# A pre-norm transformer block on one core: the softmax shift is added by two bf16 matmuls instead of four fp32r ones

## The chip, the cores and the metric

The kernel runs on one core of a Trainium2 chip. The metric is the device time of one execution in microseconds (us); lower is better. The engines are named as in the profile: PE (TensorE, matmuls), PEld (its weight loads), DVE (VectorE), ACT (ScalarE), POOL (GpSimd), SP (SyncE, which issues DMAs). Each engine runs its own instructions in program order and waits on semaphores for the others.

## What is computed

Input x is 8 sequences of 1024 positions with 128 features. Two sublayers follow each other, each on a layer norm of x and added to it.

```python
def _L0_attn_ref(x, Wq, Wk, Wv, Wo):        # 16 heads of 8, window of 64
    q = split_heads(x @ Wq); k = split_heads(x @ Wk); v = split_heads(x @ Wv)
    ...                                      # each query sees itself and the 63 keys before it
    scores = jnp.einsum('bhld,bhlwd->bhlw', q, k_win) * scale
    scores = jnp.where(invalid[None, None, :, :], -jnp.inf, scores)
    attn = jax.nn.softmax(scores, axis=-1)
    ctx = jnp.einsum('bhlw,bhlwd->bhld', attn, v_win)
    ...
    return ctx @ Wo

def _L0_ffn_ref(x, w_router, w1, w2, bias):  # 8 experts, top 2, capacity 2048 per expert
    scores = jax.nn.softmax(xf @ w_router, axis=-1)
    expert_weights, top_experts = jax.lax.top_k(scores, TOP_K)
    ...                                      # rows are gathered by expert, in order, up to the capacity
    h = jax.nn.gelu(jnp.einsum('ech,ehf->ecf', xb, w1))
    y = jnp.einsum('ecf,efh->ech', h, w2).reshape(E * capacity, hs)
    ...
    return out.reshape(sl, bs, hs) + bias

x = x + _L0_attn_ref(_layernorm(x), Wq, Wk, Wv, Wo)
x = x + _L0_ffn_ref(_layernorm(x), w_router, w1, w2, bias)
```

What matters here is the softmax. It is computed as exp(score - maximum), and the maximum has to be known before the exp.

## The kernel before

**Stages.** The eight sequences go through attention one after the other; each is eight tiles of 128 positions, and one tile is one *slot* (`slot(b, t)` on PE, DVE, ACT and POOL alike; `g` is 8b + t). Beside the slots of sequence b run the second layer norm, the routing and the scatter of sequences b-1 to b-3, cut in small steps (`small` on DVE, `sends` on POOL). After the last slot come the routing of the last sequences and then the experts, in a loop of their own.

**Units.** A slot has two *units* u = 2g and 2g+1, one for each group of 8 heads. The scores of a unit are in two PSUM banks, `sT_ps[:, u % 2, 0:2, :]`, transposed: keys in the partitions, and 1024 columns, one for each pair of query and head (128 queries, 8 heads). A unit goes through these steps:

1. `fill` (PE, L1089 and L1095; L1085 for the first tile of a sequence): a bf16 mask matmul pair writes 0 or a large negative number for the window, and four fp32 matmuls add the scores. `sT_ps` stays open for accumulation.
2. `part_max` (DVE, L675): a transposing reduce takes the maxima over blocks of 32 keys, into `kmax`, 128x32.
3. `maxima_T` (PE, L1104): two matmuls against the identity transpose `kmax` twice, to PSUM partitions 0 to 31 and 32 to 63 of `maxima_ps`.
4. `shifts` (DVE): a reduce over the key blocks with its sign turned gives `negmax` (L681), 64x32: the negative maximum of each query column, in the row of its block of queries and heads. Then `moving` (L684) is `negmax` times the 0/1 mask `blocks`, so that row c holds only the 32 columns of its own block c.
5. `shifted` (PE, L1114): four fp32r matmuls, each with 32 rows, add `moving` to the open scores. The weights `chosen` are 0/1 and pick which 8 of a bank's 16 rows go to which half of the bank, so each of them covers 256 columns.
6. `exps` (ACT, L508): exp of the two banks into `probsT`.
7. `weighted` (PE, L1124): eight matmuls with four column groups give the weighted sums and the denominators; then ACT copies them, PE transposes them (`weighted_T`, L1133), DVE divides (`normalise`, L692, L697), and PE transposes and projects (`context_T` L1138, `project` L1142). DVE adds the residual (L703).

**Order.** All orders are written out by hand. PE in a slot: `shifted(2g)`, `weighted` of the previous slot, `project`, the projections or norm transposes of a later pair, `maxima_T(2g+1)`, `fill` of unit 2g+2, `shifted(2g+1)`, `weighted`, `weighted_T`, `maxima_T(2g+2)`, in odd slots `values` (L1075), `fill` of unit 2g+3, `context_T`. DVE: `part_max(2g+1)`, side steps, residual, `shifts(2g+1)`, `part_max(2g+2)`, side steps, `normalise`, `shifts(2g+2)`. Buffers `moving`, `kmax`, `maxima_ps` and `sT_ps` are double, by u % 2.

The shift in code:

```python
for j in range(2):
    for b in range(2):
        rows = slice(b * STRIP, (b + 1) * STRIP)        # STRIP = 32
        last = mm(sT_ps[:, u % 2, b, j * 2 * P:(j + 1) * 2 * P], chosen[rows, j, :],
                  moving[rows, u % 2, :, :].rearrange("p c q -> p (c q)"),
                  start=False, stop=True, skip_group_check=True)
```

Of the kernel before, what the change touches and what calls it, by code (L numbers as in the profile page):

```python
# [5 lines left out]
F32R = mybir.dt.float32r  # L6
BF16 = mybir.dt.bfloat16
I32 = mybir.dt.int32
U32 = mybir.dt.uint32
ALU = mybir.AluOpType  # L10
ACT = mybir.ActivationFunctionType
AX = mybir.AxisListType
# [7 lines left out]
P = 128  # L20
# [8 lines left out]
HALF = P // 2  # L29
UNIT = 2 * 512  # L30
STRIP = 32
# [17 lines left out]
def moe_block_kernel(nc, x, wq, wk, wv, wo, w_router, w1, w2, bias, out):  # L49
    ctx = ExitStack()  # L50
    with ctx:
        def sb(name, shape, dt=F32):
            return ctx.enter_context(nc.sbuf_tensor(name, shape, dt))
# [4 lines left out]
        def sem(name):  # L58
            return ctx.enter_context(nc.semaphore(name))
# [17 lines left out]

        eighth = sb("eighth", [HALF, 8])
        blocks = sb("blocks", [HALF, 8, 32])
        eights = sb("eights", [HALF, 2])  # L80
        chosen = sb("chosen", [HALF, 2, P], F32R)
# [27 lines left out]
        negmax = sb("negmax", [HALF, 32])  # L109

        moving = sb("moving", [HALF, 2, 8, 32], F32R)
# [54 lines left out]
        d_rden = sem("d_rden")  # L166
        d_groups = sem("d_groups")
# [449 lines left out]
        def _(dve):  # L617
# [60 lines left out]
            def shifts(u):  # L678

                dve.wait_ge(s_maxT, u + 1)  # L680
                nc.vector.tensor_reduce(negmax[:, :], maxima_ps[u % 2][0:HALF, MAXIMA:MAXIMA + P].rearrange("p (k q) -> p q k", q=32),  # L681
                                        AX.X, ALU.max, negate=True).then_inc(s_negmax, 1)
                dve.wait_ge(s_negmax, u + 1)
                nc.vector.tensor_tensor(out=moving[:, u % 2, :, :],  # L684
                                        in0=negmax[:, :].unsqueeze(1).to_broadcast([HALF, 8, 32]),
                                        in1=blocks[:, :, :],
                                        op=ALU.mult).then_inc(s_moving, 1)
# [123 lines left out]
            for t in range(2):  # L811
# [14 lines left out]


            nc.vector.tensor_reduce(eighth[:, :], ident[0:HALF, 0:HALF].rearrange("p (x c) -> p c x", c=8),
                                    AX.X, ALU.max).then_inc(d_groups, 1)
            nc.vector.tensor_reduce(eights[:, :], ident[0:HALF, 0:96].rearrange("p (x r) -> p x r", x=2)[:, :, 0:16]  # L830
                                    .rearrange("p x (j c) -> p j x c", j=2), AX.XY, ALU.max).then_inc(d_groups, 1)
            dve.wait_ge(d_groups, 2)
            nc.vector.tensor_copy(blocks[:, :, :], eighth[:, :].unsqueeze(2).to_broadcast([HALF, 8, 32]))
            nc.vector.tensor_copy(chosen[:, :, :], eights[:, :].unsqueeze(2).to_broadcast([HALF, 2, P]))
# [222 lines left out]
        def _(pe):  # L1057
# [42 lines left out]
            def maxima_T(u):  # L1100

                pe.wait_ge(s_kmax, u + 1)
                for b in range(2):
                    last = mm(maxima_ps[u % 2][STRIP * b:STRIP * (b + 1), MAXIMA:MAXIMA + P], kmax[:, u % 2, :], ident[:, :],  # L1104
                              start=True, stop=True)
                last.then_inc(s_maxT, 1)

            def shifted(u):

                pe.wait_ge(s_moving, u + 1)  # L1110
                for j in range(2):
                    for b in range(2):
                        rows = slice(b * STRIP, (b + 1) * STRIP)
                        last = mm(sT_ps[:, u % 2, b, j * 2 * P:(j + 1) * 2 * P], chosen[rows, j, :],  # L1114
                                  moving[rows, u % 2, :, :].rearrange("p c q -> p (c q)"),
                                  start=False, stop=True, skip_group_check=True)
                last.then_inc(s_scoresT, 1)
# [268 lines left out]
```

## Time and profile before

| | us |
|---|---|
| median of 3 runs | 825.4 |
| lowest, highest | 824.17, 825.46 |
| the profiled run's own time | 825.46 |
| its span, first to last instruction | 823.7 |
| from 20 to 503 us: attention, eight sequences | 483 |
| from 503 to 548 us: last tiles, routing of the last two sequences | 45 |
| from 548 us: experts | 276 |

The three stages are cut by eye from the page's 40 slices; the first 20 us are loads and constants. "Busy" is the time in which an engine executes; matmuls and weight loads overlap, so PE and PEld are not to be added. In a row of the timeline the first number is the start in us, the second the length, then engine, line, operation, what is written and read, the shape, and how many instructions were merged; brackets give the idle time of that engine before it and what ended it.

### The profile page before, as it was taken

How to read it: one execution, taken by the hardware profiler on the slowest of the kernel's cores; microseconds unless marked ns; L12 is line 12 of the kernel's file. 1: busy time of each engine (PE TensorE's matmuls, PEld its weight loads, DVE VectorE, ACT ScalarE, POOL GpSimd, SP SyncE). 2: the span in 40 equal slices, each digit the busy share in tenths (PEclk: the TensorE clock that was granted, in tenths of full speed). 3: DMA queues.
4: the chain of work that ended last, by engine and by line, in shares of the span. 5: the costliest groups of instructions: out<-in, count | busy, mean ns of one | idle time of the engine just before them, and what ended most of it. 6: DMA issues, size and time to landing. Idle time of an engine off the chain costs nothing. (4 is left out here: it accounts for less than half of the span.)

```text
span 823.7 us, 18057 instructions
## 1 busy us (share of the span) xinstructions
PE 750.6 (91%) x7037; PEld 546.4 (66%) x7039; DVE 446.1 (54%) x1364; ACT 448.9 (54%) x923; POOL 356.4 (43%) x318
## 2 busy tenths in 40 slices
PE   6999999999999999999999997369989988989982
PEld 3566666666666666666666664227988878878872
DVE  7677777867877867867867768402212212212110
ACT  4667696686686686686685663104444333442430
POOL 3000000032233323233322354673877877877876
PEclk9999999999999999999999996569999999999997
DMA  3962000010010010010010011114455455455433
GB/s 100 367 250 61 11 15 8 8 35 25 28 32 25 29 31 25 29 31 28 25 32 24 29 49 35 54 44 123 61 88 113 62 87 111 61 87 90 59 33 32
DMA packets 49118, 50.22 MB, mean 61 GB/s; under 512 B 5905, under 2 KB 39336, under 8 KB 48016
## 3 DMA queue, kind: packets, MB, share of 16 engines
q0 software_dynamic: 22528, 17.22, 14.2%
q1 hardware_dynamic: 26512, 31.93, 12.1%
q8 instruction: 53, 0.87, 0.4%
q14 instruction: 25, 0.20, 0.1%
HBM read 17.70 MB, written 31.59 MB: 60 GB/s over the span
## 5 line engine op out<-in xcount | busy, mean ns | idle before, releaser
L432 POOL DMA_INDIRECT out<-y_sb,xg x128 | 198.5, 1551 | 67.2 <-issue 51.1
L353 POOL DMA_INDIRECT slots_dram<-rows_sb,slot_id x128 | 126.4, 987 | 208.0 <-PE sT_ps L1114 171.8
L675 DVE TRANSPOSE_TENSOR_REDUCE kmax<-sT_ps 128x32 f32<-128x1024 f32 x128 | 159.9, 1250 | 57.8 <-PE sT_ps L1095 56.9
L508 ACT ACTIVATE probsT<-sT_ps 128x1024 f32<-128x1024 f32 x128 | 132.4, 1034 | 53.2 <-PE sT_ps L1114 53.2
L607 ACT ACTIVATE hT<-sT_ps 128x512 f32<-128x512 f32 x128 | 76.5, 598 | 150.3 <-PE sT_ps L1326 142.5
L1095 PE MATMUL sT_ps<-qbd,kT 64*128 64x256 f32 x1024 | 134.4, 382 | 0.0
L1326 PE MATMUL sT_ps<-xT_hl,w_hl 128*128 128x512 f32 x384 | 102.6, 419 | 22.2 <-DVE xT_hl L1022 15.9
L1032 DVE TENSOR_TENSOR y_sb<-o_ps,xg 128x256 f32<-128x256 f32 x32 | 13.6, 425 | 184.0 <-DMA out<-y_sb,xg 95.9
L1095 PEld LDWEIGHTS sT_ps<-qbd,kT 64*128 64x128 f32 x1024 | 99.6, 193 | 10.2
L370 POOL TENSOR_TENSOR xbias<-x_sb,bias_sb 128x256 f32<-128x256 f32 x32 | 23.3, 728 | 187.3 <-PE sT_ps L1114 187.3
L1326 PEld LDWEIGHTS sT_ps<-xT_hl,w_hl 128*128 128x128 f32 x384 | 73.7, 199 | 40.7 <-DVE xT_hl L1022 16.9
L1124 PE MATMUL u_ps<-probsT,v_sb 128*32 128x128 f32 x2048 | 83.3, 281 | 0.0
L1114 PE MATMUL sT_ps<-moving,chosen 32*128 32x256 f32 x512 | 64.3, 328 | 2.2 <-DVE moving L684 1.9
L1338 PE MATMUL o_ps<-w_sb,hT 128*128 128x128 f32 x512 | 62.7, 275 | 0.0
L1338 PE MATMUL proj_ps<-w_sb,hT 128*128 128x128 f32 x512 | 62.4, 275 | 0.0
L1338 PEld LDWEIGHTS o_ps<-w_sb,hT 128*128 128x128 f32 x512 | 59.9, 192 | 0.3 <-ACT hT L607 0.2
L1124 PEld LDWEIGHTS u_ps<-probsT,v_sb 128*32 128x32 f32 x2048 | 48.5, 110 | 17.3 <-issue 0.2
L1338 PEld LDWEIGHTS proj_ps<-w_sb,hT 128*128 128x128 f32 x512 | 59.7, 192 | 0.0
L1114 PEld LDWEIGHTS sT_ps<-moving,chosen 32*128 32x128 f32 x512 | 38.2, 184 | 31.8 <-DVE moving L684 19.1
L684 DVE TENSOR_TENSOR moving<-negmax,blocks 64x256 fp32r<-64x256 f32 x128 | 53.5, 418 | 4.4
L483 ACT ACTIVATE qbd<-proj_ps,quadmask 128x256 f32<-128x256 f32 x124 | 48.6, 474 | 10.2 <-PE proj_ps L1070 10.1
L498 ACT ACTIVATE v_sb<-proj_ps 128x256 f32<-128x256 f32 (+1 forms) x124 | 37.1, 324 | 29.6 <-PE proj_ps L1075 28.9
(166 smaller groups left out, 1008.4 us busy)
## 6 DMA issues: line engine op xcount, KB each, us to landing
slots_dram<-empty_rows SPq DMA_DIRECT2D x8, 1096.0 KB, 16.3
xg<-slots_dram SPq DMA_DIRECT2D x32, 274.0 KB, 4.5
out<-xbias SPq DMA_DIRECT2D x32, 128.0 KB, 1.8
w_sb<-in_L_ffn_w SPq DMA_DIRECT2D x16, 256.0 KB, 3.1
slots_dram<-rows_sb,slot_id POOLq DMA_INDIRECT x128, 2.3
out<-y_sb,xg POOLq DMA_INDIRECT x128, 3.3
out<-empty_rows SPq DMA_DIRECT2D x1, 1024.0 KB, 25.0
x_sb<-in_L_attn_x SPq DMA_DIRECT2D x1, 896.0 KB, 5.7
```

Source lines behind the costliest of these rows:

```text
L353: pool.indirect_dma_start(out=slots_dram, out_offset=bass.IndirectOffsetOnAxis(ap=slot_id[:, g % 2, k, j:j + 1].bitcast(U32), axis=0), in_ ...
L432: pool.indirect_dma_start(out=out, out_offset=bass.IndirectOffsetOnAxis(ap=xg[:, r, 4 * c + k, ROW - 1:ROW].bitcast(U32), axis=0), in_=y_s ...
L483: nc.scalar.activation(qbd[:, p % 2, :, :, h, :].rearrange("p s b q -> p (s b) q"), bank[:, 0:2 * P].rearrange("p (c q) -> p c q", q=BLK), ...
L508: nc.scalar.activation(probsT[:, gp].rearrange("p b k h q -> p (b k h q)"), sT_ps[:, gp].rearrange("p b c -> p (b c)"), ACT.Exp).then_inc( ...
L607: nc.scalar.activation(hT[:, c % 2, f, :], hidden_ps[f], ACT.Gelu_apprx_tanh).then_inc(f_gelu, 1)
L675: nc.vector.tensor_reduce(kmax[:, u % 2, :], sT_ps[:, u % 2].rearrange("p b (c q) -> p (b c) q", q=32), AX.X, ALU.max, apply_transpose=Tru ...
L684: nc.vector.tensor_tensor(out=moving[:, u % 2, :, :], in0=negmax[:, :].unsqueeze(1).to_broadcast([HALF, 8, 32]), in1=blocks[:, :, :], op=A ...
L1095: last = mm(sT_ps[:, gp, b, blk * 2 * P:(blk + 1) * 2 * P], kT[rows, gp, at:at + P], qbd[rows, t // 2 % 2, t % 2, blk, :, :].rearrange("p ...
L1114: last = mm(sT_ps[:, u % 2, b, j * 2 * P:(j + 1) * 2 * P], chosen[rows, j, :], moving[rows, u % 2, :, :].rearrange("p c q -> p (c q)"), st ...
L1124: last = mm(sums[:, gp, :, blk, :], v_sb[:, t // 2, 2 * (t % 2) + blk, 4 * b + 2 * gp + p2, :], probsT[:, gp, b, blk, 2 * p2:2 * p2 + 2, : ...
L1326: last = mm(hidden_ps[f], w1_hl[:, r, a, f * P:(f + 1) * P], xT_hl[:, c % 2, b, :], start=(i == 0), stop=(i == 2))
L1338: last = mm(y_ps[h][:, k % 2 * D:(k % 2 + 1) * D], hT[:, c % 2, f, k * P:(k + 1) * P], w2_sb[:, r, f, :], start=(f == 0), stop=(f == FC - 1))
```

## The change

The same shift is added with other operands. `negmax` is computed on all 128 partitions: partitions 0 to 63 and 64 to 127 hold the same rows. It is then split in two bf16 parts: `negmax_hi` is its bf16 rounding, and `negmax_hl` holds the rounded value where `lowrow` is 0 and the remainder (`negmax - negmax_hi`) where `lowrow` is -1; `lowrow` is 0 or -1 by blocks of 32 partitions. `moving` becomes bf16, 16 blocks wide (512 columns), and both `blocks` and the weights, now `ones`, are bf16. Each bank takes one matmul of 64 rows, 32 with the high parts and 32 with the remainders, and 512 columns. `maxima_T` makes four transposes instead of two.

```diff
-        eighth = sb("eighth", [HALF, 8])
-        blocks = sb("blocks", [HALF, 8, 32])
-        eights = sb("eights", [HALF, 2])
-        chosen = sb("chosen", [HALF, 2, P], F32R)
+        groups = sb("groups", [P, 16], BF16)
+        blocks = sb("blocks", [P, 16, 32], BF16)
+        lowrow = sb("lowrow", [P, 1])
...
-        negmax = sb("negmax", [HALF, 32])
-
-        moving = sb("moving", [HALF, 2, 8, 32], F32R)
+        negmax = sb("negmax", [P, 32])
+        negmax_hi = sb("negmax_hi", [P, 32], BF16)
+        negmax_hl = sb("negmax_hl", [P, 32], BF16)
+
+        moving = sb("moving", [P, 2, 16, 32], BF16)
...
             def shifts(u):
 
                 dve.wait_ge(s_maxT, u + 1)
-                nc.vector.tensor_reduce(negmax[:, :], maxima_ps[u % 2][0:HALF, MAXIMA:MAXIMA + P].rearrange("p (k q) -> p q k", q=32),
+                nc.vector.tensor_reduce(negmax[:, :], maxima_ps[u % 2][:, MAXIMA:MAXIMA + P].rearrange("p (k q) -> p q k", q=32),
                                         AX.X, ALU.max, negate=True).then_inc(s_negmax, 1)
                 dve.wait_ge(s_negmax, u + 1)
+                nc.vector.tensor_copy(negmax_hi[:, :], negmax[:, :]).then_inc(d_hi, 1)
+                dve.wait_ge(d_hi, u + 1)
+                nc.vector.scalar_tensor_tensor(out=negmax_hl[:, :], in0=negmax_hi[:, :], scalar=lowrow[:, 0:1],
+                                               in1=negmax[:, :], op0=ALU.mult, op1=ALU.add).then_inc(d_hl, 1)
+                dve.wait_ge(d_hl, u + 1)
                 nc.vector.tensor_tensor(out=moving[:, u % 2, :, :],
-                                        in0=negmax[:, :].unsqueeze(1).to_broadcast([HALF, 8, 32]),
+                                        in0=negmax_hl[:, :].unsqueeze(1).to_broadcast([P, 16, 32]),
                                         in1=blocks[:, :, :],
                                         op=ALU.mult).then_inc(s_moving, 1)
...
-            nc.vector.tensor_reduce(eighth[:, :], ident[0:HALF, 0:HALF].rearrange("p (x c) -> p c x", c=8),
-                                    AX.X, ALU.max).then_inc(d_groups, 1)
-            nc.vector.tensor_reduce(eights[:, :], ident[0:HALF, 0:96].rearrange("p (x r) -> p x r", x=2)[:, :, 0:16]
-                                    .rearrange("p x (j c) -> p j x c", j=2), AX.XY, ALU.max).then_inc(d_groups, 1)
+            for b in range(2):
+                half = slice(b * HALF, (b + 1) * HALF)
+                nc.vector.tensor_reduce(groups[half, :], ident[half, half].rearrange("p (s h c) -> p h c s", s=2, h=2)[:, b, :, :],
+                                        AX.X, ALU.max).then_inc(d_groups, 1)
             dve.wait_ge(d_groups, 2)
-            nc.vector.tensor_copy(blocks[:, :, :], eighth[:, :].unsqueeze(2).to_broadcast([HALF, 8, 32]))
-            nc.vector.tensor_copy(chosen[:, :, :], eights[:, :].unsqueeze(2).to_broadcast([HALF, 2, P]))
+            nc.vector.tensor_copy(blocks[:, :, :], groups[:, :].unsqueeze(2).to_broadcast([P, 16, 32]))
+            nc.vector.tensor_reduce(lowrow[:, :], ident[:, :].rearrange("p (b h c) -> p h b c", b=2, h=2)[:, 1, :, :], AX.XY,
+                                    ALU.add, negate=True)
...
             def maxima_T(u):
 
                 pe.wait_ge(s_kmax, u + 1)
-                for b in range(2):
-                    last = mm(maxima_ps[u % 2][STRIP * b:STRIP * (b + 1), MAXIMA:MAXIMA + P], kmax[:, u % 2, :], ident[:, :],
+                for i in range(4):
+                    last = mm(maxima_ps[u % 2][STRIP * i:STRIP * (i + 1), MAXIMA:MAXIMA + P], kmax[:, u % 2, :], ident[:, :],
                               start=True, stop=True)
                 last.then_inc(s_maxT, 1)
 
             def shifted(u):
-
                 pe.wait_ge(s_moving, u + 1)
-                for j in range(2):
-                    for b in range(2):
-                        rows = slice(b * STRIP, (b + 1) * STRIP)
-                        last = mm(sT_ps[:, u % 2, b, j * 2 * P:(j + 1) * 2 * P], chosen[rows, j, :],
-                                  moving[rows, u % 2, :, :].rearrange("p c q -> p (c q)"),
-                                  start=False, stop=True, skip_group_check=True)
+                for b in range(2):
+                    rows = slice(b * HALF, (b + 1) * HALF)
+                    last = mm(sT_ps[:, u % 2, b, :], ones[rows, :], moving[rows, u % 2, :, :].rearrange("p c q -> p (c q)"),
+                              start=False, stop=True, skip_group_check=True)
                 last.then_inc(s_scoresT, 1)
```

What stands in a row on DVE in slot 0 of a steady sequence, from the residual (L703) over the first unit of `shifts` to the next `part_max`, before:

```order
L703 TENSOR_TENSOR x_sb<-tail_ps,x_sb 128x128 [waits s_att]
L681 TENSOR_REDUCE negmax<-o_ps 64x32 [waits s_maxT]
L684 TENSOR_TENSOR moving<-negmax,blocks 64x256 [waits s_negmax]
L675 TENSOR_REDUCE kmax<-sT_ps 128x32 [waits s_fill]
L759 TENSOR_SCALAR rows_sb<-rows_sb 128x8 [waits s_sent]
```

and of the changed kernel, in the same place:

```order
L710 TENSOR_TENSOR x_sb<-tail_ps,x_sb 128x128 [waits s_att]
L683 TENSOR_REDUCE negmax<-o_ps 128x32 [waits s_maxT]
L686 CAST negmax_hi<-negmax 128x32 [waits s_negmax]
L688 SCALAR_TENSOR_TENSOR negmax_hl<-negmax_hi,lowrow,negmax 128x32 [waits d_hi]
L691 TENSOR_TENSOR moving<-negmax_hl,blocks 128x512 [waits d_hl]
L677 TENSOR_REDUCE kmax<-sT_ps 128x32 [waits s_fill]
L766 TENSOR_SCALAR rows_sb<-rows_sb 128x8 [waits s_sent]
```

Nothing has moved; two instructions, each with a wait for the one ahead, stand between `negmax` and `moving`, ahead of the next transposing reduce.

PE in the same slot, from the maxima transposes to `weighted`, before:

```order
L1104 MATMUL o_ps<-ident,kmax 32x128 [waits s_kmax]
L1104 MATMUL o_ps<-ident,kmax 32x128
L1089 MATMUL sT_ps<-onehot,window 128x512 [waits s_exp]
L1089 MATMUL sT_ps<-onehot,window 128x512
L1095 MATMUL sT_ps<-qbd,kT 128x256 x4
L1114 MATMUL sT_ps<-moving,chosen 128x256 [waits s_moving]
L1114 MATMUL sT_ps<-moving,chosen 128x256 x3
L1124 MATMUL u_ps<-probsT,v_sb 32x2x64 [waits s_u,s_v_sb]
```

and of the changed kernel:

```order
L1110 MATMUL o_ps<-ident,kmax 32x128 [waits s_kmax]
L1110 MATMUL o_ps<-ident,kmax 32x128 x3
L1095 MATMUL sT_ps<-onehot,window 128x512 [waits s_exp]
L1095 MATMUL sT_ps<-onehot,window 128x512
L1101 MATMUL sT_ps<-qbd,kT 128x256 x4
L1118 MATMUL sT_ps<-moving,ones 128x512 [waits s_moving]
L1118 MATMUL sT_ps<-moving,ones 128x512
L1127 MATMUL u_ps<-probsT,v_sb 32x2x64 [waits s_u,s_v_sb]
```

The order is the same; the maxima group has two transposes more, and the shift group two matmuls less.

## Rows read from the trace of the kernel before

**Rows 1.** The page, engine shares (busy us, share, instructions) and granted clock.

```profile
PE 750.6 (91%) x7037; PEld 546.4 (66%) x7039; DVE 446.1 (54%) x1364; ACT 448.9 (54%) x923; POOL 356.4 (43%) x318
PEclk9999999999999999999999996569999999999997
```

**Rows 2.** Busy time in a stretch, attention stage; the first line names the columns.

```profile
core 0: us, PE busy (x) PEld busy (x) DVE busy (x) ACT busy (x) POOL busy (x), PEclk, DMA share, GB/s
20.00:503.00 483.00, 478.71 (x5276) 317.01 (x5276) 360.45 (x1087) 338.63 (x727) 116.57 (x126) 0.99 0.16 52
```

**Rows 3.** Timeline, PE and its weight loads, slot 0 of sequence 5.

```profile
325.90 0.14 PEld L1104 LDWEIGHTS o_ps<-ident,kmax 128*32 128x32 f32 x4 [0.17 <-issue]
...
326.25 0.39 PE L1089 MATMUL sT_ps<-onehot,window 64*128 64x512 bf16 x2
...
326.48 1.03 PE L1095 MATMUL sT_ps<-qbd,kT 64*128 64x256 f32 x8
...
327.43 0.30 PEld L1114 LDWEIGHTS sT_ps<-moving,chosen 32*128 32x128 f32 x4 [0.33 <-DVE moving L684]
...
327.86 0.38 PEld L1124 LDWEIGHTS u_ps<-probsT,v_sb 128*32 128x32 f32 x16
...
328.44 0.42 PEld L1133 LDWEIGHTS o_ps<-ident,u_sb 128*128 128x128 f32 x4 [0.20 <-issue]
...
329.02 0.14 PEld L1104 LDWEIGHTS tail_ps<-ident,kmax 128*32 128x32 f32 x4 [0.17 <-DVE kmax L675]
...
330.81 0.29 PEld L1114 LDWEIGHTS sT_ps<-moving,chosen 32*128 32x128 f32 x4
```

**Rows 4.** Timeline, DVE, the same stretch.

```profile
326.36 0.28 DVE L681 TENSOR_REDUCE negmax<-o_ps 64x32 f32<-64x128 f32 x1
326.68 0.42 DVE L684 TENSOR_TENSOR moving<-negmax,blocks 64x256 fp32r<-64x256 f32 x1
327.55 1.25 DVE L675 TRANSPOSE_TENSOR_REDUCE kmax<-sT_ps 128x32 f32<-128x1024 f32 x1 [0.45 <-PE sT_ps L1095]
...
329.70 0.27 DVE L681 TENSOR_REDUCE negmax<-tail_ps 64x32 f32<-64x128 f32 x1
330.00 0.42 DVE L684 TENSOR_TENSOR moving<-negmax,blocks 64x256 fp32r<-64x256 f32 x1
```

**Rows 5.** Timeline, second unit of slot 1: `moving` and the shift.

```profile
337.65 0.42 DVE L684 TENSOR_TENSOR moving<-negmax,blocks 64x256 fp32r<-64x256 f32 x1
...
338.89 0.30 PEld L1114 LDWEIGHTS sT_ps<-moving,chosen 32*128 32x128 f32 x4
```

**Rows 6.** Timeline, first units of slots 2 and 6: `moving` and the shift.

```profile
341.67 0.42 DVE L684 TENSOR_TENSOR moving<-negmax,blocks 64x256 fp32r<-64x256 f32 x1
342.13 0.30 PEld L1114 LDWEIGHTS sT_ps<-moving,chosen 32*128 32x128 f32 x4 [0.41 <-DVE moving L684]
...
373.25 0.42 DVE L684 TENSOR_TENSOR moving<-negmax,blocks 64x256 fp32r<-64x256 f32 x1
373.72 0.30 PEld L1114 LDWEIGHTS sT_ps<-moving,chosen 32*128 32x128 f32 x4 [0.33 <-DVE moving L684]
```

**Rows 7.** Groups by line and form: busy us, mean ns of one.

```profile
L684 DVE TENSOR_TENSOR moving<-negmax,blocks 64x256 fp32r<-64x256 f32 x128 | 53.5, 418 | 4.4
L1022 DVE TENSOR_TENSOR xT_hl<-u_ps,xT_hl 128x512 fp32r<-128x512 f32 x32 | 21.8, 681 | 30.9 <-ACT xT_hl L600 30.9
L657 DVE SCALAR_TENSOR_TENSOR rs_a<-rs_y 128x16 f32<-128x16 f32 x18 | 3.0, 167 | 0.4
L717 DVE SCALAR_TENSOR_TENSOR r_pos<-r_oh,r_sh 128x64 f32<-128x64 f32 x8 | 1.8, 225 | 0.3
```

**Rows 8.** Timeline, a side step of DVE and an indirect DMA issue of POOL.

```profile
340.19 0.98 POOL L353 DMA_INDIRECT slots_dram<-rows_sb,slot_id  x1 [2.85 <-PE sT_ps L1114]
...
340.73 0.45 DVE L646 TENSOR_SCALAR veps<-veps 128x16 f32<-128x16 f32 x1
```

More of the change, by code:

```diff
@@ L166, in moe_block_kernel @@
         d_rden = sem("d_rden")
+        d_hi = sem("d_hi")
+        d_hl = sem("d_hl")
         d_groups = sem("d_groups")
```

## The prediction

> **What bounds the kernel now.** I read four views, from the coarse to the fine. First the page's engine shares and its clock row: TensorE (PE) is busy 91% of the span, VectorE (DVE) 54%, and the clock is at full speed nearly everywhere [rows 1]. Next the stages: from 20 to 503 us, where the eight sequences go through attention, PE is busy 478.7 of 483 us and DVE 360.5, at a mean granted clock of 0.99; this is the stage that the change touches [rows 2]. PE looks like the only bound, but a busy PE may be a PE whose next matmul depends on DVE, so third, one slot in order of time. A slot is 16 heads of one tile, in two units; "half" means the time from one unit's shift matmuls to the next one's. In slot 0 of sequence 5 the first half ("odd half", 324.26 to 327.43) ends so: the maxima transposes start on PE at 325.90, DVE reduces them at 326.36, builds `moving` from 326.68 to 327.10, and the shift matmuls start at 327.43 [rows 3, 4]. The gap from the end of `moving` to the shift is 0.33 us. What the smallest gap can be, slot 2 shows, where PE waits for DVE: `moving` ends at 342.09, the shift starts at 342.13 [rows 6]. So 0.05 is the floor, and slot 0 has a cushion of 0.28 us. Slots 1, 3 and 7 repeat that gap; slots 2 and 6 have none, in slot 6 the two times are 373.67 and 373.72 [rows 6]. The fourth view is the cushion of the other unit of a slot ("even half"). In even slots it is 330.81 less 330.42, 0.39 [rows 3, 4]; in odd slots, where PE also computes the values, it is 338.89 less 338.07, 0.82 [rows 5]. So PE sets the pace, with DVE 0.3 us behind it in most odd halves and level with it in two of eight.
>
> **The change part by part.**
>
> *Shift matmuls (PE).* Four matmuls of 32 rows and 256 columns become two of 64 rows and 512 columns in bf16. The four take 0.43 us, from 327.43 to the next group at 327.86 [rows 3]. The new pair has the shape of the mask pair, which takes 0.23 (326.25 to 326.48) [rows 3]. Behind a group stands a fixed part for the change of the array's layout: `weighted` is eight matmuls in two sets of four, 0.58 (327.86 to 328.44), the two maxima transposes take 0.35 (325.90 to 326.25); if a set takes 0.23, both leave 0.12 [rows 3]. The new shift is 0.23 + 0.12 = 0.35: 0.08 less.
>
> *Maxima transposes (PE).* Two become four, in four column groups. `weighted` runs its four column groups side by side, a set in 0.23, as long as the two transposes take here, so the other two are hidden; I take 0.01 for the two more starts. Together PE saves 0.07 per unit. In odd halves the shift comes right behind the scores, which are in the same 64-row layout now, so another 0.12 is saved there, if PE is what is waited for.
>
> *Two more steps on DVE.* Between `negmax` and `moving` come a cast of 128x32 and a scalar_tensor_tensor of 128x32, each behind a wait for the one ahead. The trace has neither at this size. A scalar_tensor_tensor takes 167 ns at 128x16 and 225 ns at 128x64 [rows 7]; I take 0.19. The cast moves as little; I take 0.18, near the 167 ns. A dependent step starts 0.03 to 0.04 after the end of the last (326.36 + 0.28 to 326.68; 329.70 + 0.27 to 330.00) [rows 4]. Sum 0.19 + 0.18 + 0.05 = **0.42 us per unit**, all of it in the chain that the shift waits for. Bounds: two steps at 0.167 with no gap, 0.33, and two at 0.225 with 0.04 each, 0.53.
>
> *`negmax` on 128 partitions and not 64.* Each partition has the same 128 elements; nothing.
>
> *`moving`.* The output goes from 64x256 fp32r (418 ns) to 128x512 bf16 [rows 7]. No row has a two-input DVE operation with 16-bit operands throughout. By bytes per partition it is the row of today, 418 ns. By elements it is the 128x512 row, 681 ns, 0.26 more [rows 7]. I take 418, since it is the same line, the same repeated input and the same bytes, and keep 681 as the far end.
>
> The 681 ns row has 4-byte operands throughout. The Trainium skill ("VectorE: DVE Perf Modes", the perf-mode tier table) says that tensor_tensor takes two elements per cycle when all operands are bf16 in SBUF, and one otherwise; "Vector Engine (DVE) Microarchitecture Reference", section 5.1, says that a row read again and again keeps that mode. By that rule `moving` stays near 418 ns and the sum is the one below; by the 681 ns row the total would be 854.7.
>
> *Setup.* The masks are built once, beside loads, and the two reductions and two copies give way to three reductions and a copy. Nothing on the path; at most 1 us.
>
> *What waits behind.* The next transposing reduce on DVE (L675) is queued behind `moving`. When the shift is DVE-bound it already starts just after `moving`, without waiting for the scores, which are done by then; it takes 1.25 us [rows 4] and the next maxima transposes come 1.59 after the shift (329.02) [rows 3], so this queueing is covered by 0.2 us. ScalarE's exp follows the shift as before. The expert stage has none of these instructions.
>
> **The sum for one sequence** (16 halves; d = 0.42, cushion = gap less 0.05):
> - odd halves of slots 1, 3, 7: PE reaches the maxima 0.07 sooner, 0.28 of cushion is used up: 0.42 - 0.28 - 0.07 = +0.07 each, +0.21
> - odd half of slot 0: here DVE is itself just in time for `negmax`, so the 0.07 isn't had: 0.42 - 0.28 = +0.14; slot 4 the same, +0.14
> - odd half of slot 2: no cushion, +0.42; of slot 6: no cushion, but its chain begins with a residual that waits for PE, 0.42 - 0.08 = +0.34
> - odd half of slot 5: four more transposes stand between scores and shift, so all is hidden: -0.07
> - even halves of slots 1, 3, 4, 5, 7: cushion 0.77 or more: -0.07 each, -0.35
> - even halves of slots 0 and 6: 0.42 - 0.34 - 0.07 = 0.0; of slot 2, where side work fills DVE, about +0.13
>
> Together 1.18 - 0.22 = **+0.96 us per sequence**, 7.7 for eight. In sequences 1 to 4 slot 4 has less cushion, since more norms are computed there: +0.2 each, 0.8. The last two units have no further work of PE beside them: +0.7. Short stretches at 1.2 GHz (the stage's clock is 0.99 [rows 2]) hide the DVE chain where they fall: -1. Sum +8.2. The profiled run took 825.46 us (span 823.7 and 1.8 around it), 0.06 from the median 825.4: 825.5 + 8.2 = **833.7**.
>
> **The rivals.**
>
> *A, `moving` at one element per cycle.* 0.26 more in every half that DVE then sets, about ten of sixteen: 10 x 8 x 0.26 = 21. Time 854.7. For it: the nearest row by elements. Against: the bytes are the same. Chance 0.13.
>
> *B, the shorter matmuls win (faster).* If the two small steps cost less than the cushion, PE still sets the pace, and its savings count. Over the ten halves that DVE sets, the sum turns at an extra of 0.42 - 8.2/80 = 0.32 us per unit; below it the kernel gains. Were the steps 0.26 together, the time is 833.7 - 80 x 0.16 = 821; with DVE never the bound, 128 x 0.07 + 64 x 0.12 = 17 less, 809. For it: PE is the busier engine by far. Against: the smallest comparable step already costs 0.167 and a gap. Chance of faster 0.09; of landing within 0.2% (about what a measurement of this kernel can tell from no change) 0.09.
>
> *C, the maxima transposes don't run side by side.* Then 0.2 more per unit on PE, in front of the DVE chain in most halves: some 16 us, 850. Against: the eight matmuls of `weighted` in 0.58. Chance 0.03.
>
> *D, the cast is held up by GpSimd.* One tensor_scalar of 128x16, 167 ns elsewhere, took 450 ns at 340.73 [rows 8], beside an indirect DMA issue of GpSimd that ended at the same time. That issue starts 1.3 us after the shift at 338.89 and lasts 1 [rows 5, 8]; the new cast comes 2.4 us or more after it, behind them, except in the last sequence, where two are sent in a half: at most 16 x 0.3 = 5, 838.5. It lies in the main case's range.
>
> **How the numbers follow.** Main case 0.66, from 828.5 to 842: the low end takes 0.36 for the two steps (80 x 0.06 = 5 less), the high end 0.50 and D. A 0.13, B with no change 0.18, C 0.03. The range 827 to 855 takes in the main case, A and C, and leaves out most of B. Slower by over 0.2%: 0.82. Same: 0.09. Faster: 0.09.
>
> **What would show it.** Right: DVE busy up by about 128 x 0.37 = 47 us; the cast and the scalar_tensor_tensor near 0.18 each; `moving` near 418 ns; the gap from the end of `moving` to the shift at 0.05 in nearly all odd halves and the short even halves, where it was 0.33 and 0.39; PE waiting for `moving`; the shift group 0.35 long; odd half of slot 1 about 0.07 longer, long even halves 0.07 shorter. Wrong: `moving` near 680 (A); gaps still above 0.05 (B); the maxima group 0.5 long (C); or a low clock in more stretches than before, since PE now stands idle a little in each half, about 1.6 us for each such stretch.

## The result and the profile after

The changed kernel takes 836.4 us, the median of four runs (834.8 to 837.7), against 824.8 for the kernel before: a ratio of 1.015, with a 95% interval of 1.0128 to 1.0172. It is slower, as forecast, and 2.7 us above the 833.7 that was predicted. Its profiled execution took 842.3 us (span 840.6), 6 more than that median; a second trace of the same kernel, further down, shows which parts of it were chance.

The page's engine shares and clock row of the changed kernel, which answer to [rows 1], and under them its busy time in the attention stage, which answers to [rows 2] (the columns are those given there):

```profile
PE 737.9 (88%) x7293; PEld 519.0 (62%) x7295; DVE 499.3 (59%) x1620; ACT 449.9 (54%) x923; POOL 356.4 (42%) x318
...
PEclk9999999999999999999999997559999999999996
```

```profile
20.00:503.00 483.00, 458.97 (x5419) 285.15 (x5419) 402.66 (x1307) 333.20 (x716) 111.58 (x121) 1.00 0.15 50
```

DVE is busy 53 us longer over the span, with 256 more instructions. In the attention stage PE fell from 478.7 to 459.0 us of 483: it no longer fills the stage, it waits. For whom, the groups by line tell (busy us, mean ns of one, idle time before them and what ended it):

```profile
L691 DVE TENSOR_TENSOR moving<-negmax_hl,blocks 128x512 bf16<-128x512 bf16 x128 | 54.4, 425 | 4.4
L688 DVE SCALAR_TENSOR_TENSOR negmax_hl<-negmax_hi,lowrow,negmax 128x32 bf16<-128x32 bf16 x128 | 32.2, 251 | 4.6
L686 DVE CAST negmax_hi<-negmax 128x32 bf16<-128x32 f32 x128 | 23.3, 182 | 4.4
...
L1118 PEld LDWEIGHTS sT_ps<-moving,ones 64*128 64x128 bf16 x256 | 12.3, 93 | 59.0 <-DVE moving L691 43.5
```

The multiply that builds `moving` took 425 ns (418 was taken), the cast 182 (180 was taken), the scalar_tensor_tensor 251, where 190 was taken. PE's weight load for the shift waited 43.5 us for `moving`.

The same odd half as in [rows 3, 4], slot 0 of sequence 5, in the timeline of the changed kernel (start us, length us):

```profile
332.23 0.16 PEld L1110 LDWEIGHTS o_ps<-ident,kmax 128*32 128x32 f32 x8 [0.17 <-issue]
...
332.59 0.10 PEld L1095 LDWEIGHTS sT_ps<-onehot,window 64*128 64x128 bf16 x2 [0.20 <-issue]
...
332.73 0.29 DVE L683 TENSOR_REDUCE negmax<-o_ps 128x32 f32<-128x128 f32 x1
...
333.05 0.18 DVE L686 CAST negmax_hi<-negmax 128x32 bf16<-128x32 f32 x1
333.27 0.25 DVE L688 SCALAR_TENSOR_TENSOR negmax_hl<-negmax_hi,lowrow,negmax 128x32 bf16<-128x32 bf16 x1
333.55 0.42 DVE L691 TENSOR_TENSOR moving<-negmax_hl,blocks 128x512 bf16<-128x512 bf16 x1
...
334.03 0.10 PEld L1118 LDWEIGHTS sT_ps<-moving,ones 64*128 64x128 bf16 x2 [0.59 <-DVE moving L691]
...
334.35 0.36 PEld L1127 LDWEIGHTS u_ps<-probsT,v_sb 128*32 128x32 f32 x13 [0.23 <-issue]
```

From the start of `negmax` to the start of `moving` it is 0.82 us, where it was 0.32 [rows 4]: the chain grew by 0.50 to 0.51, not by 0.42. `moving` ends at 333.97 and the shift starts at 334.03, at the floor of 0.05, where before there were 0.33 [rows 3]. The cushion is gone, and PE waits. The four maxima transposes keep their stage of 0.36 us (332.23 to 332.59), beside 0.35 for two. The shift group is 0.32 long (334.03 to 334.35), beside 0.43 before and 0.35 in the forecast.

### The profile page after: what moved, and what is told of

Same layout as the page of the kernel before. It is cut to its first block and busy times, and to the rows that moved or that the text cites. A ratio compares the mean times of both kernels' runs of the same rounds, so it can differ in the third digit from the quotient of the medians.

```text
span 840.6 us, 18825 instructions
## 1 busy us (share of the span) xinstructions
PE 737.9 (88%) x7293; PEld 519.0 (62%) x7295; DVE 499.3 (59%) x1620; ACT 449.9 (54%) x923; POOL 356.4 (42%) x318
## 5 line engine op out<-in xcount | busy, mean ns | idle before, releaser
L677 DVE TRANSPOSE_TENSOR_REDUCE kmax<-sT_ps 128x32 f32<-128x1024 f32 x128 | 159.6, 1246 | 13.8 <-PE sT_ps L1101 13.6
L1101 PE MATMUL sT_ps<-qbd,kT 64*128 64x256 f32 x1024 | 132.5, 378 | 0.0
L1118 PE MATMUL sT_ps<-moving,ones 64*128 64x512 bf16 x256 | 50.1, 388 | 25.4 <-DVE moving L691 19.9
L691 DVE TENSOR_TENSOR moving<-negmax_hl,blocks 128x512 bf16<-128x512 bf16 x128 | 54.4, 425 | 4.4
L1118 PEld LDWEIGHTS sT_ps<-moving,ones 64*128 64x128 bf16 x256 | 12.3, 93 | 59.0 <-DVE moving L691 43.5
```

What stands on the lines that cost most here:

```text
L677: nc.vector.tensor_reduce(kmax[:, u % 2, :], sT_ps[:, u % 2].rearrange("p b (c q) -> p (b c) q", q=32), AX.X, ALU.max, apply_transpose=Tru ...
L691: nc.vector.tensor_tensor(out=moving[:, u % 2, :, :], in0=negmax_hl[:, :].unsqueeze(1).to_broadcast([P, 16, 32]), in1=blocks[:, :, :], op= ...
L1101: last = mm(sT_ps[:, gp, b, blk * 2 * P:(blk + 1) * 2 * P], kT[rows, gp, at:at + P], qbd[rows, t // 2 % 2, t % 2, blk, :, :].rearrange("p ...
L1118: last = mm(sT_ps[:, u % 2, b, :], ones[rows, :], moving[rows, u % 2, :, :].rearrange("p c q -> p (c q)"), start=False, stop=True, skip_gr ...
```

## The experiments

**Steps of the chain, one by one.** The rounded maximum is the same for all keys of a query, and the softmax doesn't depend on such a shift; so the low part can be left out, and with it one or both steps. What comes out is the same softmax, up to rounding. In both, the masks of the low rows are zero as well; the diffs leave that line and the waits out.

With no extra step (`hi_only`):

```diff
-    nc.vector.tensor_reduce(negmax[:, :], ...)
...
-    nc.vector.tensor_copy(negmax_hi[:, :], negmax[:, :])
-    nc.vector.scalar_tensor_tensor(out=negmax_hl[:, :], ...)
+    nc.vector.tensor_reduce(negmax_hl[:, :], ...)
...
```

The reduce writes `negmax_hl`, which is bf16.

> The changed kernel without its two extra VectorE steps: the negating reduce writes bf16 itself and that goes straight into `moving`; the masks of the low rows are zero. So the shift is the maximum rounded to bf16, the same for all keys of a query, and the softmax does not depend on it. The bf16 shift matmuls and the four maxima transposes stay. My theory (the loss comes from the length of the chain maxima, negmax, moving, shift, and the PE side of the change saves 0.07 us per unit and 0.12 more in odd halves): 0.28 us of cushion are back, PE sets the pace nearly everywhere, 809 to 813 us, PE waiting for `moving` almost nowhere. Rival 1 (the shorter matmuls save nothing, because the array's change of layout or the four transposes eat it): 824 to 827. Rival 2 (the wide bf16 `moving` or its longer reduce is what costs): above 830.

Measured: 809.6 us, ratio to before 0.981 (0.977 to 0.985). Rival B of the prediction had put a kernel in which DVE is never the bound at 809. The number agrees, the condition doesn't hold, as the rows below show.

With one extra step (`cast_only`), where the negmax stays f32 and one cast makes `negmax_hl`:

```diff
-    nc.vector.tensor_copy(negmax_hi[:, :], negmax[:, :])
-    nc.vector.scalar_tensor_tensor(out=negmax_hl[:, :], ...)
+    nc.vector.tensor_copy(negmax_hl[:, :], negmax[:, :])
...
```

> One extra VectorE step instead of two: negmax in f32, one cast to bf16, then `moving` (low rows masked to zero; the rounded shift is the same for all keys of a query). The prediction said that the sum turns from loss to gain at an extra of 0.32 us per unit. The cast with its gap costs 0.22. My theory: that lies inside the cushion of 0.28 in most odd halves, so only slots 2 and 6 pay: some 3 us slower than the run with no extra step, 811 to 817 us. Rival (every step in the chain costs its full length, since there is no cushion once PE is shorter): midway between the kernel with no extra step and the changed kernel, about 822 to 824.

Measured: 817.0 us, ratio 0.990 (0.986 to 0.994), at the upper edge of what was expected. In its trace the pair of halves that makes a slot grew, against no extra step, by 0.03 us in slots 1, 3 and 7, by 0.25 in slot 2 and by 0.21 in slot 6. So most slots took the step nearly for free. The gap ahead of the shift doesn't show that: in `hi_only` it is at the floor of 0.05 in 55 of the 64 odd halves (before: 13). How an odd half ends there, and what follows it (slot 1 of sequence 5):

```profile
323.85 0.42 DVE L686 TENSOR_TENSOR moving<-negmax_hl,blocks 128x512 bf16<-128x512 bf16 x1
324.32 0.10 PEld L1113 LDWEIGHTS sT_ps<-moving,ones 64*128 64x128 bf16 x2
...
324.69 1.25 DVE L677 TRANSPOSE_TENSOR_REDUCE kmax<-sT_ps 128x32 f32<-128x1024 f32 x1 [0.42 <-PE sT_ps L1096]
...
326.00 0.16 PEld L1105 LDWEIGHTS tail_ps<-ident,kmax 128*32 128x32 f32 x8 [0.22 <-DVE kmax L677]
```

The shift starts as soon as `moving` is done. But the transposing reduce waits 0.42 us for the scores, and the maxima transposes on PE start 0.06 after that reduce ends: in the even half PE waits for DVE. An odd half that ends sooner is followed by an even half that is longer. With the cast put in, the odd half of slot 1 grew by 0.22 (3.71 to 3.93) and the even half behind it shrank by 0.19 (4.11 to 3.92). So in `hi_only` DVE sets the pace of both halves in many slots, and its 809.6 is rival B's number without rival B's condition.

The steps without the PE side (`chain_only`), in the kernel before; `lowrow` holds zero here:

```diff
+    nc.vector.tensor_copy(negmax_hi[:, :], negmax[:, :])
+    nc.vector.scalar_tensor_tensor(out=negmax_hl[:, :], in0=negmax_hi[:, :], scalar=lowrow[0:HALF, 0:1],
+                                   in1=negmax[:, :], op0=ALU.mult, op1=ALU.add)
...
```

> The kernel before with only the two extra VectorE steps in its chain, on 64 partitions (cast to bf16, then a scalar_tensor_tensor with a pointer scalar of zero, so that `moving` gets the same values), and its fp32r matmuls and two transposes kept. At 0.50 us for both steps with gaps and without the savings of PE, the halves should grow by 0.22 in the odd halves of slots 0, 1, 3, 4 and 7, by 0.50 in slots 2 and 6, by 0.16 in the short even halves: 2.7 us per sequence, 22 in all: 845 to 849 us. Rival (the loss of 11 us is on the PE side: bf16 layout, four transposes): 825 to 829.

Measured: 846.0 us, ratio 1.025 (1.020 to 1.029). So the steps alone cost some 20 us, and what PE gained in the change gave back nearly half. Its odd halves of slots 0 and 1 in sequence 5 take 3.38 and 4.25 us, against 3.17 and 4.05 before: 0.20 to 0.21, what 0.49 of chain less 0.28 of cushion makes.

**Which step cost more than forecast.** Ten forms of VectorE operation, each four times, in one kernel (`forms`), among the mask building:

```diff
+            for n in range(4):
+                nc.vector.scalar_tensor_tensor(out=form_b[:, n, 0, :], in0=form_h[:, :], scalar=lowrow[:, 0:1], in1=form_x[:, :], op0=ALU.mult, op1=ALU.add)
+            for n in range(4):
+                nc.vector.scalar_tensor_tensor(out=form_b[:, n, 1, :], in0=form_h[:, :], scalar=-1.0, in1=form_x[:, :], op0=ALU.mult, op1=ALU.add)
...
```

> The changed kernel with ten forms of VectorE operation, four of each, among the mask building before the first sequence: scalar_tensor_tensor of 128x32 as in the change (bf16 and f32 in, bf16 out, pointer scalar), the same with an immediate scalar, f32 in and bf16 out, f32 throughout with immediate and with pointer, bf16 throughout; tensor_tensor 128x32 bf16 and f32 in, and bf16 throughout; and the 128x512 multiply with the repeated row in f32 and in bf16. In the changed kernel the scalar_tensor_tensor took 251 ns where 190 was forecast. Theory 1: the pointer scalar costs it; then the immediate form takes about 190 and f32 with pointer about 250. Theory 2: the 16-bit and 32-bit mix costs it; then the immediate mixed form stays at 250 and f32 throughout is near 190. Theory 3: the wait behind an operation just finished costs it; then the form of the change itself is near 190 here. The 128x512 multiply should take 425 with bf16 throughout and, if the 16-bit rate needs all operands 16-bit, near 680 with the f32 row.

The groups by line of that kernel (mean ns behind the comma; `form_h` and `form_k` are bf16, `form_x` is f32, and a form without `lowrow` has an immediate scalar or none; the type shown on the right is that of one input):

```profile
L854 DVE SCALAR_TENSOR_TENSOR form_b<-form_h,lowrow,form_x 128x32 bf16<-128x32 bf16 x4 | 0.7, 248 | 0.0
L862 DVE SCALAR_TENSOR_TENSOR form_f<-form_x,lowrow 128x32 f32<-128x32 f32 x4 | 0.7, 247 | 0.0
L860 DVE SCALAR_TENSOR_TENSOR form_f<-form_x 128x32 f32<-128x32 f32 x4 | 0.5, 184 | 0.0
L856 DVE SCALAR_TENSOR_TENSOR form_b<-form_h,form_x 128x32 bf16<-128x32 bf16 x4 | 0.5, 185 | 0.0
...
L864 DVE SCALAR_TENSOR_TENSOR form_b<-form_h 128x32 bf16<-128x32 bf16 x4 | 0.5, 186 | 0.0
...
L870 DVE TENSOR_TENSOR form_m<-form_x,form_k 128x512 bf16<-128x512 f32 x4 | 2.5, 684 | 0.0
L872 DVE TENSOR_TENSOR form_m<-form_h,form_k 128x512 bf16<-128x512 bf16 x4 | 1.4, 419 | 0.0
```

Theory 1 holds: the pointer scalar costs 63 ns, with one bf16 and one f32 input as with f32 throughout, and the mix of types nothing. Theory 3 falls, since the form of the change takes 248 ns here too. The time of this kernel, 846.0 in a single run, says nothing. The last two rows settle rival A as well: the same multiply takes 684 ns when the repeated row is f32 and 419 when both inputs are bf16. The Trainium skill ("VectorE: DVE Perf Modes", the perf-mode tier table) gives two elements per cycle for tensor_tensor only with all operands bf16; both rows agree with it.

Then the same in the kernel (`immediate`), with both steps kept (the masks of the low rows are zero here too):

```diff
-    nc.vector.scalar_tensor_tensor(out=negmax_hl[:, :], in0=negmax_hi[:, :], scalar=lowrow[:, 0:1],
+    nc.vector.scalar_tensor_tensor(out=negmax_hl[:, :], in0=negmax_hi[:, :], scalar=0.0,
...
```

> The changed kernel with both extra steps kept, but the scalar_tensor_tensor takes the immediate 0.0 in place of the pointer scalar (the masks of the low rows are zero, so `moving` holds the maximum rounded to bf16 and the softmax is unchanged). Among ten forms measured in one kernel the immediate one took 185 ns and the one with the pointer 248. The slope between the kernels with one and with two extra steps is 19.4 us for 0.28 us per unit, 69 us per us. Theory: 0.063 x 69 = 4.4 us less than the changed kernel's 836.1 to 836.4: 831 to 833 us, near the forecast of 833.7, which had used 0.19 for this step. Rival (the step's length is hidden behind the wait for its own semaphore): 836.

Measured: 831.7 us, ratio 1.009 (1.006 to 1.012). The step took 193 ns there, and the time is 4.4 to 4.7 us below the changed kernel's 836.1 and 836.4. With the step at the length that the prediction had given it, the kernel lands 2 us below the predicted time.

**Shape or type.** The kernel before, with two transposes and four shift matmuls of 256 columns, and only the types changed (`small_bf16`):

```diff
-        blocks = sb("blocks", [HALF, 8, 32])
...
-        chosen = sb("chosen", [HALF, 2, P], F32R)
-        negmax = sb("negmax", [HALF, 32])
-        moving = sb("moving", [HALF, 2, 8, 32], F32R)
+        blocks = sb("blocks", [HALF, 8, 32], BF16)
+        chosen = sb("chosen", [HALF, 2, P], BF16)
+        negmax = sb("negmax", [HALF, 32], BF16)
+        moving = sb("moving", [HALF, 2, 8, 32], BF16)
```

> The kernel before in its own shapes (two transposes, 64x256 `moving`, four shift matmuls of 32 rows and 256 columns), with only the type changed: the reduce writes bf16, and masks, `moving` and `chosen` are bf16. No extra step. From 425 ns at 128x512 and about 170 at 128x32 the multiply of 256 elements should take 285 ns in place of 418: the chain is 0.13 us shorter, worth it only in slots 2 and 6 where PE waits for it. If what PE saves in the change comes from the shapes (half the matmuls, rows laid out as the scores are), this kernel gains only that: 822 to 824 us. If it comes from the type (fp32r to bf16, as in the weight loads, 183 ns against 92), the shift group falls from 0.43 to 0.3 and the time goes to 808 to 814, level with the kernel without extra steps.

Measured: 810.4 us, ratio 0.985 (0.980 to 0.990). The prediction had worked PE's saving out of shapes and layouts; it is the type. The groups and the timeline of this kernel (sequence 5, the shift that ends the even half of slot 0):

```profile
L684 DVE TENSOR_TENSOR moving<-negmax,blocks 64x256 bf16<-64x256 bf16 x128 | 36.3, 283 | 4.4
...
L1114 PEld LDWEIGHTS sT_ps<-moving,chosen 32*128 32x128 bf16 x512 | 14.4, 92 | 31.3 <-issue 16.7 <-DVE moving L684 8.1
```

```profile
319.92 0.11 PEld L1114 LDWEIGHTS sT_ps<-moving,chosen 32*128 32x128 bf16 x4
...
320.24 0.27 PEld L1124 LDWEIGHTS u_ps<-probsT,v_sb 128*32 128x32 f32 x12 [0.21 <-issue]
```

Four bf16 matmuls of 32 rows and 256 columns take the 0.32 us that two of 64 rows and 512 columns take in the changed kernel. A weight load takes 92 ns where in the kernel before this row said, with the same count:

```profile
L1114 PEld LDWEIGHTS sT_ps<-moving,chosen 32*128 32x128 f32 x512 | 38.2, 184 | 31.8 <-DVE moving L684 19.1 <-issue 6.2
```

In this kernel PE waits for `moving` 8.1 us in all, and `moving` takes 283 ns in place of 418. That the shorter `moving` isn't the reason for the gain, slot 1 shows: there the shift had a cushion of 0.28 us already before, and the slot still went from 8.07 to 7.85 us, 0.11 for each unit, which is what the shift group lost.

**The cushion, tested on that kernel.** The same two steps, on 64 partitions and with the immediate scalar (`small_two`):

```diff
+    nc.vector.tensor_copy(negmax_hi[:, :], negmax[:, :])
+    nc.vector.scalar_tensor_tensor(out=negmax_hl[:, :], in0=negmax_hi[:, :], scalar=0.0,
+                                   in1=negmax[:, :], op0=ALU.mult, op1=ALU.add)
...
```

> The kernel in the shapes of before and in bf16 (810.4 us) with the same two extra steps in its chain, immediate scalar, on 64 partitions; about 0.43 us more per unit. Its odd halves showed 0.47 us from the end of `moving` to the shift, 0.42 above the floor. Theory of the cushion: in slots 0, 1, 3 and 7 the two steps fit into it and cost nothing, and only slots 2, 4 and 6 pay (0.40, 0.25 and 0.29 in the odd halves, up to 0.3 in the even ones): 1.4 us per sequence, 820 to 824 us. Rival (a longer chain costs its length wherever it stands, 69 us per us as in the changed kernel): 838 to 842.

Measured: 819.6 us, ratio 0.996 (0.993 to 0.999), just under what was expected; the ten runs spread from 816.5 to 824.9. Here 0.42 us more of chain costs 9 us, where in the shapes of the change 0.44 us cost 22 (809.6 to 831.7). Odd halves of sequence 5 against `small_bf16`: slot 0 from 3.06 to 3.09, slots 1, 3 and 7 by 0.01, slot 2 from 3.10 to 3.52, slot 6 from 3.96 to 4.24, slot 4 from 3.16 to 3.23. Nearly all of it is paid in slots 2 and 6, where there was little or no cushion (gaps of 0.05 and 0.19 in `small_bf16`, against 0.46 in slot 1).

**A theory that fell.** In the first trace of the changed kernel the even half of slot 2 takes 3.8 to 4.1 us in sequences 3 to 7, and 3.46 in sequence 1, and in that half the transposing reduce behind the shift starts late. GpSimd issues two indirect DMAs in the half before it. The kernel with one of them moved (`sends_apart`):

```diff
-            following = [(0, 0), (0, 1), (1, 0), (1, 1), (2, 0), (2, 0)]
+            following = [(0, 0), (0, 1), (1, 0), (1, 1), (2, 0), (2, 1)]
```

> The changed kernel with one number changed: of the two indirect DMA issues that GpSimd makes back to back in the first half of slot 2, the second goes to the other half. In the changed kernel's trace the transposing reduce behind the shift starts 0.38 us or more late in slot 2 of sequences 3 to 7, and the even half of slot 2 takes 3.8 to 4.1 us there against 3.46 in sequence 1. Theory: the second issue holds the matmuls' signal back; with one issue per half the even half of slot 2 is near 3.5 in all sequences, and the time 2 us lower (834 to 835). Rival (side work on VectorE in that half makes it late): the halves stay at 3.8 to 4.1 and the time at 836.4.

Measured: 839.9 us (835.7 to 842.7), ratio 1.016 (1.011 to 1.021). The half shrank to 3.63, but the time did not fall to the 834 to 835 that the theory asked for. And the second trace of the changed kernel, with nothing moved, shows why the first finding can't be read as a success:

> The changed kernel once more, for a second trace of it. Its first profiled execution took 842.3 us, 6 more than the median of its other runs. Theory: the part after the last shift (slot_id to the last send, 5 us longer than the attention accounts for) holds chance stalls, and is 4 to 5 us shorter here; the delayed transposing reduces in slot 2 of sequences 3 to 7 come back in the same places, 0.2 to 0.5 us each. Rival: the late tail belongs to the change and comes back as well; then the profiled execution is again near 842.

Measured: 836.1 us, and the profiled execution 838.1. The waits of the transposing reduce L677 for the scores, in slot 2 of sequence 5, in the first trace of the changed kernel:

```profile
349.38 0.39 PE L1118 MATMUL sT_ps<-moving,ones 64*128 64x512 bf16 x2 [0.61 <-issue]
349.69 1.25 DVE L677 TRANSPOSE_TENSOR_REDUCE kmax<-sT_ps 128x32 f32<-128x1024 f32 x1 [0.36 <-PE sT_ps L1101]
```

and in the second:

```profile
350.51 1.24 DVE L677 TRANSPOSE_TENSOR_REDUCE kmax<-sT_ps 128x32 f32<-128x1024 f32 x1
...
350.65 0.39 PE L1118 MATMUL sT_ps<-moving,ones 64*128 64x512 bf16 x2 [0.61 <-DVE moving L691]
```

In the second trace the reduce starts ahead of the shift, without a wait, and the even half of slot 2 is 3.58 to 3.60 from sequence 2 on. GpSimd makes its two issues there all the same. So the late signal was a matter of that execution, and the theory that two issues hold it back isn't supported; what was expected of this second trace, that the late reduces come back, was wrong. The stretch from the last shift to the end of the span was 325.6 us in the first trace and 322.9 in the second (before: 320.5), so about half of the late tail was chance too. What held the signals back in the first trace stays open.

## Why the prediction was right, and where it was off

- **What bounds the kernel.** Right. That PE is busy 91% doesn't say that it sets the pace; the 0.33 us between the end of `moving` and the shift [rows 3, 4] did, and `chain_only` bears the cushion of 0.28 out. Once the chain was longer than the cushion, the time grew with it. The kernels with extra steps of 0, 0.22, 0.44 and 0.50 us took 809.6, 817.0, 831.7 and 836.4: 34 us per us of chain at first, then about 65; the last two lie too close to tell their slope from that one (4.7 us for 0.06). The line between the second and the third crosses 824.8, the kernel before, at 0.34 us; the prediction had put the turning point at 0.32.
- **The cast.** 182 ns, 180 was taken.
- **The scalar_tensor_tensor.** This is the term that was mis-sized: 251 ns against 190. The rows that I took between, L657 and L717 [rows 7], gave the right price for the immediate form (185), and the pointer scalar on top was missed. It made d 0.51 in place of 0.42; the pointer alone is 4.4 to 4.7 us, by `immediate`.
- **The odd halves.** In slots 1, 3 and 7 they grew by 0.16 us, in slot 0 by 0.16, in slot 2 by 0.51 and in slot 6 by 0.41. The prediction's own formula with d = 0.51 gives 0.16, 0.23, 0.51 and 0.43. Slot 0 is off by 0.07: there PE's saving was had after all. Slot 4, taken to be like slot 0, grew by 0.28 in sequence 5.
- **The even halves.** In even slots the prediction took 0.39 for the gap throughout. That is slot 0; the trace of before has 0.17 in slot 2, 0.83 in slot 4 and 0.24 in slot 6. In slots 0 and 6, where it forecast no change, they grew by 0.07 and 0.08, in slot 2 by 0.22 and not 0.13.
- **What PE saves.** The sum was right by luck, its parts were not. The shift group went from 0.43 to 0.32, not to 0.35, and it is the bf16 type that does it, not the shape. The 0.12 per odd half for a layout that need not change was mostly not there: slot 1 (both halves) takes 7.82 us in `hi_only`, with the 64-row layout, and 7.85 in `small_bf16`, without it. The odd half alone is shorter, 3.71 against 3.94, but the even half behind it is longer, 4.11 against 3.91, by the wait for the transposing reduce shown above. Two wrong parts, 0.07 x 2 + 0.12 = 0.26 for a slot, and 0.25 was measured (8.07 to 7.82 in slot 1).
- **The maxima transposes.** Right; rival C fell, 0.36 us for the group against the 0.5 that would have shown it.
- **`moving`.** Right; 425 ns. Rival A fell, and the 684 ns row shows that it would have been the truth with one f32 operand.
- **The cast held up by GpSimd (D).** Fell: all 128 casts have a mean of 182 ns.
- **The clock.** The prediction let 1 us go for short stretches at 1.2 GHz, in which the chain is hidden, and feared more of them in the changed kernel. The feared rise isn't seen. In the profiled execution of before the granted clock fell to 1.2 GHz for 3.4 us at 309.2, 432.1 and 493.5, in slot 6 of sequences 4, 6 and 7; in the first two the odd half took 5.63 us and not 4.06; in the first trace of the changed kernel there was none between 80 and 503 us, in the second one, in slot 6 of sequence 2. But `sends_apart`, whose chain is that of the changed kernel, has three again. Single traces can't say which kernel has more. That such a stretch hides the chain is seen in `chain_only`: where the clock is low in slot 6 of sequence 4, the odd half takes 5.64 us with the two steps, against 5.63 without. The stretch of the second trace, behind the row ahead of it (columns as in [rows 2]):

```profile
188.00:191.40 3.40, 3.40 (x41) 2.63 (x38) 1.62 (x3) 2.14 (x5) 0.82 (x1) 1.00 0.02 5
191.40:194.80 3.40, 3.40 (x22) 2.07 (x23) 2.02 (x8) 0.37 (x1) 0.16 (x1) 0.50 0.06 21
```

In the row ahead of the fall PE is busy for all of its 3.40 us, at full clock. Each such stretch costs 1.2 to 1.6 us by the halves around it.

**Why the number came so near.** In part by luck. With d = 0.51 the prediction's sum is 0.09 x 80 = 7 us higher, 841, and the median was 836.4. Of the 4.5 us between, 1.7 are in the halves: sequence 5 grew by 1.65 us (60.68 to 62.33 in the second trace) where the formula with 0.51 gives 1.86, mainly since slot 0 kept PE's saving and the long even halves gained 0.10 and not 0.07. The other 2.8 are shown only in part. The timed runs have no trace, but a mean granted clock each: 0.950 over 32 runs of the kernel before, 0.953 over 21 of the changed one. That makes 82 and 79 us at the lower clock, a difference of about one such stretch, so perhaps 1.5 us. Between the two traces there are also terms that the forecast had at nothing or small: the time up to the first shift was 1.5 us shorter in the second trace of the changed kernel, and the stretch behind the last shift 2.5 longer, where the forecast had 0.7. How much of these is chance stays open.

Rival B, the faster outcome, was right in that PE's work can be shortened: some 15 us come out as soon as the two steps leave the chain. Its condition, that DVE is then never waited for, holds nearly in `small_bf16` (6 of 64 odd halves at the floor) and not in `hi_only` (55 of 64).

**A better kernel.** `hi_only` (809.6) and `small_bf16` (810.4) beat both kernels, by 1.9% and 1.5% of the kernel before in their own runs. The shift of a softmax needs no low part. The second has more room: its chain is 0.14 us shorter, and it takes two further steps at 9 us where the first takes them at 22.

## What to carry to other kernels

Measure the gap between the end of what an engine waits for and its start, half by half, before trusting its busy share: the cushion there (0.28 us here) is what a longer chain may cost for free, and what shortens the other engine eats it too. Then look one wait further: in `hi_only` that gap was gone and yet a step of 0.22 us cost 0.03 for a slot, since the next wait took back what the first had lost. Only the time of a whole slot tells. Before splitting a value in two for the sake of its precision, ask whether the precision is needed; here a shift that cancels was carried in two parts at the price of 0.51 us of chain per unit. And price an operation by a row with the same kind of operands, scalars included, not only with the same shape.

## What the runs showed of the hardware

- A scalar_tensor_tensor with a pointer scalar takes 63 ns more than with an immediate (248 against 185 at 128x32 with one bf16 and one f32 input, 247 against 184 with f32 throughout); in the kernel it is 251 against 193.
- A tensor_tensor of 512 elements per partition takes 419 ns with both inputs bf16 and 684 with one f32 input; of 256 elements 283 in bf16 and 418 in fp32r.
- A weight load of 128 columns takes 92 ns in bf16 (32 rows) or 93 (64 rows), and 184 in fp32r with 32 rows. The matmul groups behind them shrank from 0.43 to 0.32 us.
- The granted clock fell to 1.2 GHz for 3.4 us in the middle of work, at times in the same slot of other sequences, in some executions and not in others of the same kernel.
- The spread between runs of one kernel goes with that clock: of 32 runs of the kernel before, those with a mean granted clock of 0.942 to 0.946 took 825.9 to 827.6 us, those with 0.956 to 0.958 took 820.8 to 821.5.
